# Attention scores of two heads per step, with 64-row matmuls for the keys' low parts, in a fused attention and mixture-of-experts kernel

## The reference, cut to what matters

```
xn = layer_norm(x)                                  # x: 4 x 2048 x 256
q, k, v = xn' @ Wq, xn' @ Wkv                       # xn' = layer_norm(xn) * g; 8 heads of 64, one k and v for all heads
q, k = 4 * q / |q|, 4 * k / |k|
out = softmax(q @ k.T) @ v                          # per batch of 2048 rows and head
s = layer_norm(out @ Wout) * out_g
f = silu(ffn(xn))                                   # top-2 routing over 8 experts, 256 -> 1024 -> 256, gelu
result = x + s * f
```

## Time and profile before

| what | value |
|---|---|
| median of 3 runs | 3015.31 us (3010.92 to 3015.75) |
| profiled execution, its time | 2982.51 us |
| profiled execution, its span | 2980.7 us |
| mean granted TensorE clock | 0.986 |
| busy over the span | PE 95%, PEld 67%, DVE 69%, ACT 64%, POOL 35% |
| chain that ended last | PE 70%, DVE 11%, issue 7%, ACT 5%, POOL 5% |

### The profile page before, as it was taken

The page is one execution under the profiler, slowest core; times in us unless marked ns, Lnnn a source line. Parts: engine busy times, 40 slices in busy tenths (PEclk is TensorE's granted clock), DMA queues, the critical chain, the costliest instruction groups (busy, mean ns, idle before and its releaser), DMA issues.

```text
span 2980.7 us, 86161 instructions
## 1 busy us (share of the span) xinstructions
PE 2832.3 (95%) x38213; PEld 2000.1 (67%) x38277; DVE 2066.8 (69%) x2883; ACT 1904.8 (64%) x2363; POOL 1030.7 (35%) x662
## 2 busy tenths in 40 slices
PE   4999999998999989999999999999999999999996
PEld 3666667666766756766667676677666666666674
DVE  6878787889987853334333433358899899898976
ACT  5666666765766655556565655557666676666764
POOL 2333333331888510000000000025555656555544
PEclk8999999999999999999999999999999999999998
DMA  3122222100433111221211221111111111111101
GB/s 107 58 92 83 101 70 98 51 27 30 150 117 111 39 31 56 73 66 64 86 61 57 87 73 57 36 38 31 40 47 48 47 47 49 43 46 45 35 24 46
DMA packets 111014, 184.13 MB, mean 62 GB/s; under 512 B 12648, under 2 KB 78128, under 8 KB 110640
## 3 DMA queue, kind: packets, MB, share of 16 engines
q1 hardware_dynamic: 98352, 145.04, 14.9%
q0 software_dynamic: 12288, 33.57, 3.4%
HBM read 92.58 MB, written 85.98 MB: 60 GB/s over the span
## 4 chain that ended last, share of the span: by engine, by line
PE 70%; DVE 11%; issue 7%; ACT 5%; POOL 5%; DMA 1%; SPq 0%; DVEq 0%; POOLq 0%; ACTq 0%
PE pair L581 20%; PE bank L656 14%; PE pair L642 14%; PE bank L603 5%; PE bank L611 5%; PE bank L601 5%; DVE arena L1147 5%; ACT arena L802 4%; POOL routed_rows L1224 3%; PE bank L565 2%; PE bank L524 2%; PE bank L626 1%; POOL w_lo L1252 1%; DVE q_n L1070 1%; POOL q_small L1196 1%
## 5 line engine op out<-in xcount | busy, mean ns | idle before, releaser
L1147 DVE TENSOR_TENSOR arena<-arena 128x1024 bf16<-128x1024 f32 x854 | 1123.3, 1328 | 231.1 <-ACT arena L802 227.1
L802 ACT ACTIVATE arena<-pair 128x1024 f32<-128x1024 f32 x1024 | 1038.7, 1023 | 380.4 <-PE pair L581 379.7
L581 PE MATMUL pair<-qT,kT 128*128 128x512 f16 x4096 | 1060.8, 382 | 55.1 <-ACT arena L802 53.2
L1265 POOL TENSOR_TENSOR arena<-arena 128x1024 bf16<-128x1024 f32 x170 | 352.3, 2072 | 1375.0 <-ACT arena L802 1369.6
L601 PEld LDWEIGHTS bank<-vhl,arena 128*128 128x128 bf16 x8192 | 590.7, 99 | 121.5 <-issue 2.8
L603 PE MATMUL bank<-vhl,arena 128*128 128x64 bf16 x8192 | 651.3, 195 | 0.0
L601 PE MATMUL bank<-vhl,arena 128*128 128x65 bf16 x8192 | 649.2, 193 | 0.0
L603 PEld LDWEIGHTS bank<-vhl,arena 128*128 128x128 bf16 x8192 | 551.8, 98 | 121.5 <-issue 2.8
L581 PEld LDWEIGHTS pair<-qT,kT 128*128 128x128 f16 x4096 | 340.5, 98 | 314.2 <-ACT arena L802 62.2
L818 ACT ACTIVATE h_f<-pair,b1T 128x512 f32<-128x512 f32 x320 | 219.4, 686 | 332.9 <-PE pair L642 332.9
L656 PE MATMUL bank<-w_hl,arena 128*128 128x256 bf16 x3840 | 425.7, 273 | 0.6 <-DVE att L1163 0.6
(11 more groups left out here) (191 smaller groups left out, 2382.7 us busy)
## 6 DMA issues: line engine op xcount, KB each, us to landing
routed_rows<-h_f SPq DMA_DIRECT2D x80, 256.0 KB, 3.8
att<-routed_rows SPq DMA_DIRECT2D x40, 512.0 KB, 4.4
expert_rows<-att SPq DMA_DIRECT2D x40, 512.0 KB, 2.9
raw<-in_L_ffn_w SPq DMA_DIRECT2D x32, 512.0 KB, 4.2
xn_rows<-s_hl SPq DMA_DIRECT2D x16, 512.0 KB, 2.9
xT_out<-xn_rows SPq DMA_DIRECT2D x64, 128.0 KB
w_lo<-in_L_attn_x SPq DMA_DIRECT2D x64, 128.0 KB, 2.1
out<-w_lo SPq DMA_DIRECT2D x64, 128.0 KB, 2.0
```

Source lines behind the costliest of these rows:

```text
L581: t = nc.tensor.matmul(pairs[n % 2][:, i * BANK:(i + 1) * BANK], kT[b % 2][:, part, kb * P:(kb + 1) * P], qT[g % 2][:, h, :], start=(part ...
L802: nc.scalar.activation(p_f32[:, n % NP, :], pairs[n % 2][:, :], ACT.Exp).then_inc(exped, 1)
L1147: nc.vector.tensor_tensor(p_lo[:, n % NP, :], p_f32[:, n % NP, :], p_top[:, n % NP, :, 1], ALU.subtract).then_inc(lowed, 1)
L1265: nc.gpsimd.tensor_tensor(p_lo[:, n % NP, :], p_f32[:, n % NP, :], p_top[:, n % NP, :, 1], ALU.subtract).then_inc(lowed_pool, 1)
```

## The change

A step now covers **two heads and one block of 128 keys for each**. `halves(n)` gives for half `i` of a step the group, head and key block. Half 0 is an even head; half 1 is the odd head next to it, and it runs `BEHIND` = 4 steps behind: it takes key block `kb - 4` when the even head takes `kb`. The number of steps grows by 4 at each of the two attention stretches (1032 in all), and in the first 4 and last 4 steps of a stretch only one half is at work; `columns(n)` gives ScalarE, VectorE and GpSimd that half's 512 columns.

In `scores(n)` the matmul with the keys' low part uses 64 rows: rows 0 to 63 for the even head and rows 64 to 127 for the odd head. For this `qhl` is laid out anew, so that the query's high part stands in rows 0 to 63 of `qT` for an even head and in rows 64 to 127 for an odd one. The product of the two low parts is no longer formed. The order of the four matmuls is both full ones and then both 64-row ones in an even step, and the reverse in an odd step; `main` issues `scores(a)` and `scores(a + 1)` together when `a` is even.

`LAG` is 3, and odd steps are weighed one slot later, so that after a couple of `scores` two `weigh` follow. `weigh(n)` now waits for `low(n)` ahead of its first matmul. Two heads add up at the same time, so there are three accumulator banks, and only one side bank is left. In the experts the second half of the gathered rows' transposes goes into the third accumulator bank. `O_AT` stands one slot later, `S_AT` nine slots earlier.

```diff
@@ -22,7 +22,8 @@
-LAG = 4
+LAG = 3
+BEHIND = 4
@@ -126,8 +127,8 @@
     def attention_slots(first, end):
-        for n in range(first, end + LAG):
-            slots.append(("att", n if n < end else None, n - LAG if n - LAG >= first else None))
+        for n in range(first, end + LAG + 1):
+            slots.append(("att", n if n < end else None, n - LAG if first <= n - LAG < end else None))
@@ -142,17 +143,27 @@
+    weighed_in = [[] for _ in slots]
...
-            place["weigh", b] = at
+            if b is not None:
+                place["weigh", b] = at + b % 2
+                weighed_in[at + b % 2].append(b)
...
-    base = [place["scores", STEPS * g] for g in range(NG)]
+
+    def first_step(g):
+        return STEPS * g + (BEHIND if g > XG else 0)
+
+    def steps_to(g):
+        return first_step(g) + STEPS + BEHIND
+
+    base = [place["scores", first_step(g)] for g in range(NG)]
...
-    S_AT = [3 * g for g in range(BG)] + [base[0] + 24 * (g - BG) + 12 for g in range(BG, NG)]
+    S_AT = [3 * g for g in range(BG)] + [base[0] + 24 * (g - BG) + 3 for g in range(BG, NG)]
@@ -164,7 +175,7 @@
-            O_AT.append(base[g + 1] + 16 * j + 9)
+            O_AT.append(base[g + 1] + 16 * j + 10)
@@ -179,10 +190,21 @@
-    def step(n):
-        hh, pr = divmod(n, NPAIR)
+    def halves(n):
+        late = n >= CUT
+        for i in range(2):
+            at = n - BEHIND * i - (CUT if late else 0)
+            if 0 <= at < (NG - XG - 1 if late else XG + 1) * STEPS:
+                g, rest = divmod(at, STEPS)
+                yield i, g + (XG + 1 if late else 0), 2 * (rest // KB) + i, rest % KB
+
+    def columns(n):
+        active = [i for i, _, _, _ in halves(n)]
+        return slice(active[0] * BANK, (active[-1] + 1) * BANK)
+
+    def last_step(hh):
...
-        return g, h, pr, hh
+        return first_step(g) + h // 2 * KB + KB - 1 + BEHIND * (h % 2)
@@ -202,9 +224,9 @@
-        acc_banks = banks[0:2]
+        acc_banks = banks[0:3]
...
-        side_banks = [b[:, :] for b in banks[2:4]]
+        side_banks = [banks[3][:, :]]
@@ -247,14 +269,16 @@
-        qhl = sb("qhl", [P, H, 2, DH], F16)
+
+        qhl = sb("qhl", [P, H // 2, 4, DH], F16)
+        q_his, q_los = qhl[:, :, 0:4:3, :], qhl[:, :, 1:3, :]
...
-        oden = sb("oden", [P, GT, 1], F32)
+        oden = [sb(f"oden{i}", [P, GT, 1], F32) for i in range(2)]
@@ -568,33 +593,36 @@
             def scores(n):
-                g, h, pr, _ = step(n)
-                b = g // BG
-                pe.wait_ge(qT_copied, GT * (g + 1))
-                pe.wait_ge(kT_copied, BG * b + 2 * pr // GT + 1)
+
+                for _, g, _, kb in halves(n):
+                    pe.wait_ge(qT_copied, GT * (g + 1))
+                    pe.wait_ge(kT_copied, BG * (g // BG) + kb // GT + 1)
                 if n == CUT:
...
                 pe.wait_ge(exped, n - 1)
-                for i in range(2):
-                    kb = 2 * pr + i
-                    for part in range(2):
-                        t = nc.tensor.matmul(pairs[n % 2][:, i * BANK:(i + 1) * BANK],
-                                             kT[b % 2][:, part, kb * P:(kb + 1) * P], qT[g % 2][:, h, :],
-                                             start=(part == 0), stop=(part == 1))
+                for turn in range(2):
+                    for i, g, h, kb in halves(n):
+                        into, keys = pairs[n % 2][:, i * BANK:(i + 1) * BANK], slice(kb * P, (kb + 1) * P)
+
+                        part = (turn + n) % 2
+                        rows = slice(i * DH, (i + 1) * DH) if part else slice(0, P)
+                        t = nc.tensor.matmul(into, kT[g // BG % 2][rows, part, keys], qT[g % 2][rows, h, :],
+                                             start=(turn == 0), stop=(turn == 1))
                 t.then_inc(scored, 1)
             def weigh(n):
-                g, h, pr, hh = step(n)
-                b, s, bank = g // BG, n % NP, acc_banks[hh % 2]
-                V = vhl[b % 2]
+                s = n % NP
                 pe.wait_ge(exped, n + 1)
-                pe.wait_ge(v_split, BG * b + 2 * pr // GT + 1)
+                pe.wait_ge(*low_done(n))
                 if n == CUT:
                     pe.wait_ge(y_done, FG * GT)
-                if pr == 0:
-                    pe.wait_ge(divided, hh - 1)
-                for i in range(2):
-                    kb = 2 * pr + i
+                    pe.wait_ge(xgT_copied, 2 * FG)
+                for i, g, h, kb in halves(n):
+                    b, hh = g // BG, g * H + h
+                    V, bank = vhl[b % 2], acc_banks[hh % 3]
+                    pe.wait_ge(v_split, BG * b + kb // GT + 1)
+                    if kb == 0:
+                        pe.wait_ge(divided, hh - 2)
                     for qb in range(GT):
@@ -602,9 +630,6 @@
-                pe.wait_ge(*low_done(n))
-                for i in range(2):
-                    kb = 2 * pr + i
@@ -616,9 +641,14 @@
-                    bank, free = side.take(xgT_copied, 2 * fg + half + 1)
+                    if half:
+                        bank = acc_banks[2][:, :]
+                        pe.wait_ge(divided, (XG + 1) * H)
+                        pe.wait_ge(xgT_copied, 2 * fg)
+                    else:
+                        bank, free = side.take(xgT_copied, 2 * fg + 1)
+                        pe.wait_ge(*free)
...
-                    pe.wait_ge(*free)
@@ -665,10 +695,12 @@
                         side.banks = [s for s in side.banks if any(s[0] is bank for bank in side_banks)]
-                    if a is not None:
+
+                    if a is not None and a % 2 == 0:
                         scores(a)
-                    if b is not None:
-                        weigh(b)
+                        scores(a + 1)
+                    for n in weighed_in[clock.now]:
+                        weigh(n)
                 elif kind == "turn":
@@ -799,7 +831,7 @@
-                nc.scalar.activation(p_f32[:, n % NP, :], pairs[n % 2][:, :], ACT.Exp).then_inc(exped, 1)
+                nc.scalar.activation(p_f32[:, n % NP, columns(n)], pairs[n % 2][:, columns(n)], ACT.Exp).then_inc(exped, 1)
@@ -1125,10 +1157,11 @@
-                acc = acc_banks[hh % 2][:, 0:GT * (DH + 1)].rearrange("p (j n) -> p j n", j=GT)
-                yield from clock.at(place["weigh", hh * NPAIR + NPAIR - 1] + 1)
-                dve.wait_ge(weighed, (hh + 1) * NPAIR)
-                nc.vector.reciprocal(oden[:, :, :], acc[:, :, DH:DH + 1]).then_inc(head_inv, 1)
+                acc = acc_banks[hh % 3][:, 0:GT * (DH + 1)].rearrange("p (j n) -> p j n", j=GT)
+                yield from clock.at(place["weigh", last_step(hh)] + 1)
+                dve.wait_ge(weighed, last_step(hh) + 1)
+                dve.wait_ge(divided, hh - 1)
+                nc.vector.reciprocal(oden[hh % 2][:, :, :], acc[:, :, DH:DH + 1]).then_inc(head_inv, 1)
@@ -1262,7 +1296,8 @@
-                nc.gpsimd.tensor_tensor(p_lo[:, n % NP, :], p_f32[:, n % NP, :], p_top[:, n % NP, :, 1],
+                c = columns(n)
+                nc.gpsimd.tensor_tensor(p_lo[:, n % NP, c], p_f32[:, n % NP, c], p_top[:, n % NP, c, 1],
```

27 lines of the change are left out of this document (14 added, 13 removed).

## The result

The changed kernel takes 3019.07 us (median of 20 runs, 3011.49 to 3021.77) against 3010.94 us for the kernel before (20 runs, 3003.97 to 3018.42): a ratio of 1.0024, with a 95% interval of 1.0016 to 1.0031. It is slower by a quarter of a percent, where 2.8% faster was forecast. The profiled execution took 3019.07 us, span 3017.3 us, mean granted clock 0.969 (before: 0.986).

A forecast was written before the change was run, and what follows sets the result against it. TensorE was taken as the bound: pace 1771.1, waits 120 and ends 3 us make 1894 for the attention stretches in place of 1979.5, so 2897 us, times 1.011 gives 2930 us; range 2845 to 3065 us.

The forecast's parts named there:

- The pace: TensorE's own time without waits in both attention stretches, forecast to fall from 1908.7 to 1771.1 us.
- d: Price of one change between full and 64-row matmuls on TensorE, taken as 0.08 us, 82.6 us for 1032 changes.
- the list of waits: TensorE's waits listed in the earlier profile's two attention stretches, 70.8 us, subtracted from 1979.5 to get its own pace.
- Rival 1: Row changes in the scores cost nothing and VectorE is the bound: 2895 us, or 2795 with waits unchanged; chance 0.18.
- rival 2: The two 64-row score matmuls run in turn, so nothing is saved: 3102 us; chance 0.07.
- rival 3: Each row change in the scores drains the array, 0.167 or 0.265 us each: 3020 or 3122 us; chance 0.17.
- What it does to the waits: Step pricing TensorE's waits in both stretches, from VectorE's load, earlier waits for `low` and one side bank: 120 us.
- The prediction's own signs: Attention-stretch checks: couple 1.45 us, wrong over 1.6; PE waits, wrong past 170 us; `low` and bank waits under 60.
- The ceiling: VectorE can fill at most 90.6% of the attention stretches, so they last 1858 us, 87 over TensorE's pace.
- The one bank: One side bank for the projections in place of two, waits put at 0.5 us a tile, 32 us.
- The base: Whole kernel's starting profile at 2982.5 us, its forecast of 2897 us scaled by 1.011 to the runs' median.
- Rival 4: `low` and the one side bank hold up TensorE in the stretches, 220 us of waits: 3030 us; chance 0.08.

The follow-up runs named there:

- e13: Kernel before with coupled steps, 64-row matmuls and one head per step, plus the changed kernel's one side bank, three accumulators and tables: 3005.39 us, 0.9988 of before.
- e5: Kernel before with scores and weighings in couples and 64-row matmuls for the keys' low parts, one head per step, two side banks: 2986.92 us, 0.9923 of before.
- e9: Changed kernel with `low` on VectorE and GpSimd for only 512 of a step's 1024 columns: 2883.08 us, 0.9526 of before.
- e10: Changed kernel with both `low` and the exponential on only 512 of a step's 1024 columns: 2859.86 us, 0.9450 of before.
- e15: Kernel before with `low` for only 512 of a step's 1024 columns: 2939.38 us, 0.9763 of before.
- e4: Kernel before with 64-row matmuls for the keys' low parts in each step, one head per step, no couples: 2974.91 us, 0.9976 of before.

## Why the prediction was wrong

**The pace: right in kind, too big in size.** The matmuls run side by side, as taken; d was put at 0.08 and is 0.095 to 0.10 measured, far from the 0.163 at which it would decide. Over both stretches the pace falls from 1870 to 1769 us, 101 less, where 137.6 was forecast: the dearer changes (1032 x 0.02 = 20 us), and 16 us for the extra half steps and small distances. That 1769 is so near to the forecast 1771.1 is luck: the starting value of 1908.7 held some 39 us of short halts and clock losses that the list of waits doesn't show. The d of 0.08 is luck too. It took the mean distance of two starts for the surplus of a change; the single starts are 5.09, 5.22 and 5.40 us, so the change costs 0.05 us more than the distance before it. The halving for a slow TensorE has no support in the granted clock, which was 1.00 there.

Rival 1's free changes (d = 0), rival 2 (in turn) and rival 3 (a full drain of 0.167) are out. Rival 3's 3020 us is the measured time, but by another mechanism. The Trainium skill's rule that a change of tiling mode drains TensorE (TensorEngine Tiling (Array Packing), Key Properties) agrees in kind: there is a price, at each change. It is 0.095 to 0.10 us, less than the 0.167 to the end of a matmul's record; whether it is a drain no run shows.

**The step that failed is "What it does to the waits", with its 120 us in place of 70.8.** By the distances, halts go from 83 to 197 us in the two stretches, and the clock takes 47 us in place of 16: 145 us more, against 101 of pace. The profile of before is from a fast chip. Some 28 of the 145 us are the chip's (3010.9 less 2982.5), which leaves, as an estimate, 117 us for the change where 49 was forecast. The kernel then gains 101 us by the pace and 7 in the experts and loses 117 by halts and clock: 9 us slower, and 8 was measured. So the waits account for 68 us of the miss and the size of the pace for 36.

The list of waits, which the prediction reads, sees only a part: PE's waits in it grow from 70.8 to 157 us, 79 of them for the exponential. The prediction's own signs did not show the failure. A couple takes 1.51 us (under 1.6), PE's waits stay under 170, and those for `low` and for the bank at L548 and L590 are 42 us, under 60 as said. Three things were wrong.

- *The ceiling.* VectorE was to be filled to 90.6% of the stretches; it is busy for 83% of them in the changed kernel (85% before), while it binds more. Its share of busy time was the wrong measure: it waits for exponentials for 300 us itself (227 before), and part of its busy time is `low` drawn out beside GpSimd. The run with half of `low` (84 us in one stretch, against 34 in the kernel before) shows VectorE and GpSimd together as the cause, and ScalarE's wait for VectorE (71.9 to 14.1 us) shows the way through ScalarE's queue. That it is the length of VectorE's bursts against the lead of the others that counts, and that couples cut that lead, is my reading; no run varies either alone.
- *The one bank* was priced at what stands at its own waits, 32 us. Those are small (21 us in all, at L531, L548, L578, L590), yet e13 against e5 shows 19 us for one stretch, as waits for the exponential further on. Which of the bank and the tables does it stays open.
- *The clock* was left out. It takes 47 us in place of 16, some of it perhaps the chip's: 0.969 granted on average in place of 0.986. Runs with few halts lose least (0 to 2 us in the second stretch of e9, e10 and e15), but runs with about 100 us of halts lose between 4 and 16, so halts alone don't set it.

**The base was one of the fast chips.** The pace and the waits were taken from a profile at 2982.5 us, and the sum scaled by 1.1%. In the one profile of a slower chip the surplus is waits for "issue" and clock losses in the scatters' steps of the first stretch, not a factor on all.

Rival 4, that the waits eat it (220 us, 3030 us), came nearest, with 0.08 given to it. Its sum is near that by the distances (244 us with the clock); its mechanism came only in part, since it named `low` and the one side bank, which hold 42 of PE's 157 us of waits, and not the exponential.

## What to carry to other kernels

Two 64-row matmuls on different halves of the array cost one, but each change between full and half rows costs 0.1 us: one couple of 512 columns between two changes pays for them and hardly more (8 us of 2983 in e4), two couples gain 0.22 us.

When TensorE gets faster in a pipeline of several in-order engines, price the next engine by an experiment that halves its load, not by its share of busy time. Here the halving of `low` gave back 34 us of a stretch in a kernel with VectorE at 87%, and 84 in one with it at 85%. Work moved to another engine is not yet relief: 26 fewer `low` on VectorE left its busy time where it was.

An edit that is free by itself (one bank less) is not free in another order; test it in the order in which it will run.

## What the runs showed of the hardware

- Two 64-row matmuls of 512 columns in different rows and PSUM banks start 3 to 4 ns apart.
- A change of rows costs 95 to 96 ns going in, behind 512 columns as behind 65, and 92 to 103 ns going out, plus 10 ns at the next matmul. The first weight load behind a change starts 4 ns before its own matmul.
- VectorE's 128x1024 float32 subtraction takes 1.21 us on average while GpSimd does nothing, and 1.55 us, up to 3.99, beside a tensor operation of GpSimd.
- The same kernel takes 2983, 3010, 3023 or 3026 us on different chips, and the surplus looked into sits in waits for "issue" of TensorE while GpSimd's scatters run (25 us of it in one profile).
